# VectorE's order inside a group of the scatter stage: both sets of one-hots ahead of the weighing of the rows

## The reference, cut to what matters

```python
# layer 2: softmax over each node's incoming edges, then a weighted sum of the sources' rows
ex = jnp.exp(logits - seg_max[dst])
a = ex / seg_sum[dst]
rst = jax.ops.segment_sum(soft_label[src] * a[:, None], dst, num_segments=N)
# layer 3: degrees, and two rounds of x <- A x with the counts of edges between nodes
deg = jax.ops.segment_sum(jnp.ones(r.shape), r, num_segments=n)
w = dinv[r] * dinv[c]
x = jax.ops.segment_sum(w[:, None] * x[c], r, num_segments=n)
# layer 4: a gate of every edge from its 40 attributes
gate = jax.nn.silu(edge_attr @ W1.T + b1) @ W2.T + b2
```

## Time and profile before

| | us |
|---|---|
| median of three runs | 6890.07 |
| the profiled execution | 6896.36 |
| its span | 6894.1 |
| PE, PEld busy over the span | 3935.5, 3010.7 |
| DVE, ACT, POOL busy over the span | 4076.4, 2562.1, 3949.5 |
| stretch with quads, 3010 to 5700 us: DVE, POOL, PE busy | 1662.02, 1445.67, 1547.33 |
| stretch without quads, 5700 to 5830 us: DVE, PE busy | 120.19, 81.28 |

### The profile page before, as it was taken

How to read it: one execution, slowest core, us unless ns; L and a number is a source line. 1 busy time by engine, 2 the same in 40 slices (tenths; PEclk the granted TensorE clock), 3 DMA queues, 4 the chain that set the end, 5 groups by cost and what they waited for, 6 DMA issues and landing times.

```text
span 6894.1 us, 121916 instructions
## 1 busy us (share of the span) xinstructions
PE 3935.5 (57%) x46612; PEld 3010.7 (44%) x46613; DVE 4076.4 (59%) x7184; ACT 2562.1 (37%) x5259; POOL 3949.5 (57%) x3993
## 2 busy tenths in 40 slices
PE   6455555545545554355555555556555565887775
PEld 5344444323323323134444444444444444776774
DVE  4444444555555556345566666566666568667999
ACT  1111111111111111244455445445445445776664
POOL 2566666666666666655555555555555553225996
PEclk8555555555555555555555555555555555999998
DMA  3455422222222222133333233333333332667886
GB/s 128 166 159 165 122 48 47 49 53 48 48 47 48 48 48 46 30 52 55 56 57 59 54 57 55 56 57 57 55 58 56 55 57 53 190 186 172 193 191 132
DMA packets 1414672, 571.31 MB, mean 83 GB/s; under 512 B 1069539, under 2 KB 1353711, under 8 KB 1413953
## 3 DMA queue, kind: packets, MB, share of 16 engines
q1 hardware_dynamic: 1309185, 452.39, 29.4%
q0 software_dynamic: 104896, 110.96, 7.3%
HBM read 394.81 MB, written 168.16 MB: 82 GB/s over the span
## 4 chain that ended last, share of the span: by engine, by line
another core or an unknown queue 23%; PE 18%; issue 16%; ACT 16%; DVE 13%; DMA 9%; SPq 2%; POOL 1%; DVEq 0%; ACTq 0%; POOLq 0%
DMA rb<-dst_rows 6%; PE ps L1250 4%; ACT rb L1606 3%; ACT meta_b L1616 3%; DMA meta_b<-blocks 3%; DVE ps L2099 2%; ACT meta_a L1538 2%; PE ps L1288 2%; PE ps L1421 2%; ACT rb L1636 2%; ACT at_table L1636 2%; PE ps L1210 2%; ACT meta_b L1623 1%; PE ps L1238 1%
## 5 line engine op out<-in xcount | busy, mean ns | idle before, releaser
L928 POOL DMA_INDIRECT by_src<-meta_a,row_src x1612 | 1609.5, 998 | 1343.2 <-DVE meta_a L2354 922.6
L917 POOL DMA_INDIRECT ring<-h_table,meta_b x1616 | 1641.9, 1016 | 945.8 <-issue 452.7
L1523 ACT ACTIVATE ring<-ring,meta_b 128x48 f32<-128x48 f32 x1616 | 386.4, 322 | 2142.1 <-DMA ring<-h_table,meta_b 2104.3
L1421 PE MATMUL ps<-dst_i,meta_b 128*128 128x128 bf16 x2450 | 398.7, 295 | 901.5 <-ACT rb L1636 331.5
L1250 PE MATMUL ps<-ring,WX 128*128 128x48 bf16 x2188 | 440.2, 235 | 559.7 <-DVE row_src L2230 331.3
L2593 DVE TENSOR_TENSOR meta_b<-big,ps 128x1152 bf16<-128x1152 bf16 x546 | 734.5, 1346 | 0.0
L1421 PEld LDWEIGHTS ps<-dst_i,meta_b 128*128 128x128 bf16 x2450 | 229.6, 152 | 1133.1 <-issue 1107.3
L1250 PE MATMUL ps<-row_src,WX 128*128 128x48 bf16 x4376 | 502.5, 233 | 261.5 <-issue 260.1
L1380 PE MATMUL ps<-WX,meta_b 128*128 128x49 bf16 (+1 forms) x14742 | 591.4, 200 | 61.0 <-issue 28.2
L1250 PEld LDWEIGHTS ps<-ring,WX 128*128 128x128 bf16 x2188 | 358.7, 164 | 591.7 <-DVE row_src L2230 343.3
L1288 PE MATMUL ps<-meta_a,w1T 40*48 40x256 f32 x806 | 401.6, 596 | 358.6 <-DMA meta_a<-in_attrT 179.1
(11 more groups left out here) (343 smaller groups left out, 9058.7 us busy)
## 6 DMA issues: line engine op xcount, KB each, us to landing
meta_b<-blocks SPq DMA_DIRECT2D x490, 144.0 KB
by_src<-default SPq DMA_DIRECT2D x44, 1456.0 KB
meta_a<-by_src SPq DMA_DIRECT2D x273, 216.0 KB, 4.4
rb<-lo_rows SPq DMA_DIRECT2D x202, 256.0 KB
rb<-src_rows SPq DMA_DIRECT2D x273, 144.0 KB
rb<-dst_rows SPq DMA_DIRECT2D x273, 144.0 KB
meta_a<-in_attrT SPq DMA_DIRECT2D x402, 80.0 KB
ring<-h_table,meta_b POOLq DMA_INDIRECT x1616
```

The costliest lines, as they stand in the source:

```text
L917: pool.indirect_dma_start(ring[:, gg % RING, j, 0:width], None, table, bass.IndirectOffsetOnAxis(ap=index(g * GROUP + j), axis=0)) \
L928: pool.indirect_dma_start(by_src, bass.IndirectOffsetOnAxis(ap=row_src[:, t:t + 1], axis=0), rec[:, q % RECS, j, :], None).then_inc(s_sc[q ...
L1421: mm = pe.matmul(bank(5, P, at=i * P), ohS_n[:, a % 3, :, u * TRIO + i], ohK_n[:, a % 2, u * TRIO + i, :], start=True, stop=True)
L1523: scaled = act.activation(row, row, ACT.Copy, scale=meta_b[:, t, M_NORM:M_NORM + 1])
```

## The change

`attend_rows(n)` is split. Its first half, the degrees of group n, becomes `attend_degrees(n)` and stays where it was. `build_K(n - 2)` and `build_S(n - 2)` come next. The second half, the weighing of group n's rows with its two waits, comes after them, and `collect` stays last. No instruction, wait or buffer is added or taken away.

```diff
-                def attend_rows(n):
+                def attend_degrees(n):
 
                     dve.wait_ge(s_rowc, bucket_of(n) + 1)
                     dve.wait_ge(s_oha, n + 1)
...
                         dve.tensor_reduce(cell_of[:, n * SG:(n + 1) * SG],
                                           ohT_n[:, n % 3, :].rearrange("p (j n) -> p j n", n=P), AX_X, ALU.add) \
                             .then_inc(s_deg, 1)
+
+                def attend_rows(n):
+
                     by = ex_d[:, n * SG:(n + 1) * SG][:, :, None].to_broadcast([P, SG, EW])
                     dve.wait_ge(s_ng, taken(n))
...
                     if n < SGROUPS:
-                        attend_rows(n)
+                        attend_degrees(n)
                     if 0 <= n - 2 < SGROUPS:
                         build_K(n - 2)
                         build_S(n - 2)
+                    if n < SGROUPS:
+                        attend_rows(n)
                     if 0 <= n - 4 < SGROUPS:
                         collect(0, n - 4, V)
```

## The result

The changed kernel takes 7034.41 us (median of four runs, 7030.99 to 7037.71) against 6889.84 us for the kernel before beside it: a ratio of 1.0215, 95% interval 1.0193 to 1.0238. It is 145 us slower, above the whole range of the prediction (6840 to 6938). All the times of one comparison are from one chip; chips differ (the kernel before took 6788 to 6897 us beside the experiments), so the experiments are told as ratios to the kernel before on their own chip.

The account below looks back on a forecast made before the run. The pace was taken to be a ring of scatters, late take, counts and gate, without VectorE's one-hots. Terms of 3 + 4 + 1 = 8 us off 6890.07 gave 6882 us; range 6840 to 6938.

Parts of the forecast that it names:

- What bounds the stretch: Stretch with quads: scatters delay TensorE's take, then counts, gate and next burst; VectorE has only 0.76 us in this ring.
- K and S ahead of the rows, first and second term: TensorE's direct waits for VectorE, 3 us off (bounds 0 and 7); rows' waits in stretch without quads, 4 us off.
- K and S beside scatters: Building one-hots inside the scatter burst would not lengthen scatters (0.97 us either way); priced at nought.
- The gates earlier, third term: Records on time at VectorE's gates, 172 late places, 205 us; 1 us off, bounds 48 us slower and 42 faster.
- the fitted line: Next gate's time against lateness: falls 0.40 us per us where a group follows, rises 0.15 where none does.
- company alone: Argument against the slower rival: a long turn is followed by a short one with or without VectorE, so lateness isn't cause.
- The slower one: On-time records start the burst before the take gets through: up to 48 us slower, 6938 us; chance 0.25.
- Its own sign: ScalarE's "remote" waits (1135 us) growing would show the slower rival right.
- The faster one: Earlier records start scatters earlier, backlogs end earlier, the take's long waits shorten: 42 us more off, 6840 us; chance 0.33.
- The change doesn't do what it says: VectorE, loaded anyway, isn't on time at the gates; only the first two terms remain, within the likeliest case (0.42).
- The two stretches' lengths stay: Sign expected: stretches with quads (2690 us) and after the last quad (130 us) keep their lengths while VectorE's waits move.
- no take began to wait for the rows: Had TensorE's take begun to wait for VectorE's rows, the prediction would have been wrong altogether.
- scatters beside K or S still take 0.97 us: Had a scatter beside the one-hots' building become longer than 0.97 us, the prediction would have been wrong altogether.

Follow-up runs that it names:

- Without K: Kernel before with K built for the first two groups only, so later edge counts use stale one-hots: ratio 1.0194.
- the take ahead of the burst: GpSimd waits for the same place's take before each quad's scatters, from the 35th quad: 0.9512 in the kernel after, 0.951 in the kernel before.

## Why the prediction was wrong

**What bounds the stretch** fits the runs: a ring of burst, held take, counts and gate, without VectorE's one-hots in it. With one scatter of four the ring opens, and the stretch with quads shrinks from 2699 to 1898 us in the order of before.

**K and S ahead of the rows, first and second term.** The waits moved as said: rows from 631 to 331 us (I said about 240; the takes behind a backlog are held longer), gates 414 us up. TensorE's direct waits for VectorE did not stay under 7 us: for S they are 13.5 us, 9 more than before (those for the gates, 2.5 us, are gone from the list). The stretch without quads gave nothing that can be seen. These two terms, 7 us off in the sum, brought about nought, small against what follows.

**K and S beside scatters**, priced at nought: borne out. Without K, in the order of before, the loss is there, and with the take ahead of the burst, or one scatter, the two orders agree within 0.2%. The Trainium skill ("SBUF — State Buffer", section "Who interferes with whom") says that TensorE never waits for another engine's access, which would make the scatters' moment indifferent to the take. That does not come out of the trace, though it doesn't show an access that waits either. The holds of 4.70 us (mean), which fall to 0.01 us (median) when three of four scatters are left out, show a coupling between scatters and TensorE's completions. By what path, no run here shows.

**The gates earlier, third term: this step failed.** The mechanism was in the prediction (a late burst catches less of the take), and so were both group means, 9.24 us after 51 places on time and 7.56 us after the late ones. But it set a loss of 48 us by the fitted line against a gain of up to 42 and put the term at 1 us off. By its own measure, from the end of the gate's matmuls to the end of the next ones, the runs show three things in its place.

- Where the next place has a group too: +89 us, where the line had 48. Lateness ahead of these places fell by some 109 us, so each us of it cost 0.8 us and not 0.40. The difference of the means errs as far the other way: 101 x 1.68 = 170 us.
- Where the next place has none: 26 us faster, where the line had 13. The sign was right.
- One place further, where a place with a group follows one without: +70 us, half of the loss. The prediction looked only as far as the next gate and had no term for it. There the take stands behind two bursts, which now hold it to their end in 65 of 70 cases instead of 30 of 69. Why they do so now is not shown.

Nor was the slope company alone ("a long turn of the ring is followed by a short one"): without K, with VectorE's work taken away rather than reordered, the places of the first type take 8.43 us by the same measure, against 8.12 before and 8.71 after. That trace is from a chip on which the kernel before is about 100 us faster, so the step there is probably larger.

**The rivals.** The slower one was the right mechanism, at 0.25 and with a price of 48 us; the stretch lost 135, nearly three times as much. Its own sign was named and came: ScalarE's "remote" waits grew by 228 us. The faster one is refuted: the waits behind backlogs did not shorten, 93 of the takes stand behind one after and 94 before, and they are held for 7.56 us instead of 6.31. "The change doesn't do what it says" is refuted by the 5 late places. The range failed because its upper end was the slower rival's price by the slope, for the next place alone; its own two means would have put that end at 7060. "The two stretches' lengths stay" failed with it, by the 135 us; no take began to wait for the rows, and scatters beside K or S still take 0.97 us (296 cases).

**What I held to be the theory** was itself corrected by the runs: I took the burst's start against the take for all of it. It explains half of the longer holds of after against before; the other half stands behind backlogs. But the stream also lets takes through in its pauses, wherever they lie, and that is worth more (5.8%) than the order ever cost (2.1%).

The fastest of all kernels here that compute everything is the kernel with two memsets of 128x416 ahead of each burst, 0.942 in either order; the one that says openly what it does, the wait for the take, is 0.951.

## What to carry to other kernels

When a step off the critical path is made earlier, ask what its result starts, and beside what that then runs: here records 0.9 us earlier set off the scatters ahead of the take instead of behind it, and less waiting at the gates made the kernel 2% slower. If groups of places in the trace already show the condition that the change makes the rule (here 51 places on time against 101 late), work out the price both by a line through them and by the difference of their means (here 48 and 170 us, measured 89), let one rival carry the larger, and look past the next place: half of the loss here came one place later. And where a burst of GpSimd's indirect DMAs runs beside short waits on TensorE's semaphores, try a wait that puts the matmuls first, or a pause between bursts (1.2 us did most here, 0.7 us next to nothing), before touching anything else.

## What was unexpected of the hardware

Takes whose matmuls are recorded as done wait for their semaphore while scatters of 0.97 us run one every 1.27 us. In the kernel after, the number of scatters that start between a take's recorded end and its semaphore is 2 in 137 cases, 4 in 69, 6 in 17, and odd in only 14 of 243. That is no rule of such streams: in the kernel before it is odd in 62 of 242, with two memsets in 82 of 239. Behind the last scatter it comes after 0.9 us (median, in the kernel with two memsets). The recorded end is modelled, so whether the matmuls themselves or only their completions are late stays open. A pause of 0.74 us between bursts brings 1% or less, one of 1.24 us 5.8%. And a scatter that lies wholly beside the building of K or S takes 0.97 us, as elsewhere, but one beside the adding up of the degrees (L2623) 1.10 us in the mean (90 cases in after).
